# Attention loop without the turned outputs and the output product, in a vision transformer block on one core

## The reference, cut to what matters

```python
h = rows
q, k, v = split(layernorm_rows(h) @ [Wq Wk Wv].T)          # 16 heads of 16
q, k = layernorm16(q) * gq + bq, layernorm16(k) * gk + bk
att = softmax(where(causal, q @ k.T, -1e30)) @ v
h1 = h + att @ Wo.T + bo                                    # what the kernel adds
z = layernorm(h1) * gamma + beta
pre = z @ [abel_w, gate_w] + bias                           # 256 + 8 columns
top2 = the two best of 8 experts, softmax of their logits
moe = sum over top2 of weight * (gelu(z @ ew1[e] + eb1[e]) @ ew2[e] + eb2[e])
moe = moe @ expm(gens[0]) @ expm(gens[1]) @ expm(gens[2])   # gens: 3 of 256 x 256
out = residual + gelu(pre) and moe mixed by a sigmoid gate
```

## Time and profile before

| | us |
|---|---|
| median of 3 runs | 359.7 (358.9 to 361.76) |
| the profiled execution | 359.24 |
| its span | 356.7 |
| busy PE | 320.9 (90% of the span) |
| busy DVE | 219.9 (62%) |
| busy ACT | 184.6 (52%) |
| busy POOL | 140.8 (39%) |

### The profile page before, as it was taken

How to read it: one execution, slowest core, us unless ns; L and a number is a source line. 1 busy time by engine, 2 the same in 40 slices (tenths; PEclk the granted TensorE clock), 3 DMA queues, 4 the chain that set the end, 5 groups by cost and what they waited for, 6 DMA issues and landing times.

```text
span 356.7 us, 6514 instructions
## 1 busy us (share of the span) xinstructions
PE 320.9 (90%) x1954; PEld 272.7 (76%) x1954; DVE 219.9 (62%) x590; ACT 184.6 (52%) x432; POOL 140.8 (39%) x147
## 2 busy tenths in 40 slices
PE   5999999729999999987989599999999999998794
PEld 4987556528888888875778498899988999986673
DVE  0275467997789999987888478776322212113674
ACT  0212455846688989855423785243434556550451
POOL 2001815041445665373004248757752644522000
PEclk9999999955799999999999999999999999999999
DMA  8571411123111110009622366535442567641443
GB/s 253 195 275 55 187 56 56 55 91 131 48 47 48 47 46 17 2 1 408 237 90 80 95 210 178 174 108 169 131 157 75 180 193 194 200 137 59 144 145 103
DMA packets 21120, 45.29 MB, mean 127 GB/s; under 512 B 2086, under 2 KB 14436, under 8 KB 20836
## 3 DMA queue, kind: packets, MB, share of 16 engines
q1 hardware_dynamic: 17444, 36.79, 31.3%
q0 software_dynamic: 2496, 6.82, 6.2%
q10 hardware_dynamic: 1152, 1.32, 1.2%
HBM read 37.71 MB, written 7.22 MB: 126 GB/s over the span
## 4 chain that ended last, share of the span: by engine, by line
PE 71%; issue 7%; DMA 6%; DVE 5%; SPq 3%; ACT 3%; POOL 3%; DVEq 0%; POOLq 0%; ACTq 0%
PE banks L1573 11%; PE banks L1582 10%; PE banks L1515 9%; PE banks L1289 7%; PE banks L1430 6%; PE banks L1406 5%; SPq L372 3%; PE banks L1334 3%; PE banks L1448 3%; PE banks L1379 3%; PE banks L1393 3%; DMA qk_sb<-y_rows 3%; PE banks L1486 2%; DMA qn_sb<-z_rows,gidx_sb 2%; PE banks L1417 2%
## 5 line engine op out<-in xcount | busy, mean ns | idle before, releaser
L1573 PE MATMUL banks<-qn_sb,w_sb 128*128 128x128 f32 x416 | 51.1, 276 | 1.2 <-ACT qn_sb L671 1.0
L1573 PEld LDWEIGHTS banks<-qn_sb,w_sb 128*128 128x128 f32 x416 | 48.6, 192 | 2.1 <-ACT qn_sb L671 1.2
L1582 PE MATMUL banks<-w_sb,sq_sb 128*128 x208 | 49.0, 379 | 0.0
L671 ACT ACTIVATE qn_sb<-banks,col_sb 128x128 f32<-128x128 f32 x52 | 21.0, 454 | 43.9 <-PE banks L1560 39.8
L1204 DVE TENSOR_TENSOR pT_sb<-banks,p_sb 128x256 f32<-128x256 f32 x26 | 11.0, 424 | 52.0 <-PE banks L1582 45.9
L484 POOL DMA_INDIRECT y_rows<-pT_sb,sidx_sb x26 | 25.7, 990 | 43.4 <-DVE pT_sb L1204 42.5
L1582 PEld LDWEIGHTS banks<-w_sb,sq_sb 128*128 128x128 f32 x208 | 38.1, 190 | 4.4
L682 ACT ACTIVATE sq_sb<-banks,col_sb 128x128 f32<-128x128 f32 x104 | 32.3, 364 | 16.4 <-PE banks L1573 13.7
L478 POOL DMA_INDIRECT qn_sb<-z_rows,gidx_sb x26 | 27.9, 1073 | 20.5 <-PE banks L1560 11.5
L572 ACT ACTIVATE kc_sb<-banks,col_sb 32x152 f32<-32x152 f32 x66 | 31.0, 470 | 1.1
L1289 PE MATMUL banks<-patch_sb,wtok_sb 128*128 128x252 f32 (+1 forms) x120 | 26.1, 380 | 4.3 <-DMA wtok_sb<-in_w_tok 4.3
(11 more groups left out here) (234 smaller groups left out, 635.2 us busy)
## 6 DMA issues: line engine op xcount, KB each, us to landing
w_sb<-in_w SPq DMA_DIRECT2D x26, 512.0 KB
...
```

Source lines behind the costliest of these rows:

```text
L1573: last = nc.tensor.matmul(bank[2 + 2 * s + c // 2][:, (c % 2) * 128:(c % 2 + 1) * 128], w1_sb[:, w0:w0 + 128], xsT_sb[:, (2 * s + k) * 128 ...
L1582: last = nc.tensor.matmul(bank[6 + s][:, 0:D], hidT_sb[:, s * HID + k * 128:s * HID + (k + 1) * 128], w2_sb[:, ds(e * 4 * D + k * D, D)], ...
```

## The change

- **The loop** no longer turns attention outputs and makes no output product, up to step 8. GpSimd writes each tile's attention output into `h1_sb`, where it stays; `turn_att`, `keep_attT`, `output` and `finish` of tiles 0 to 2 stand in steps 9 and 10, and those of the other eight behind the loop, between the normalised rows and `pre` of the first tiles. Two buffers hold turned outputs, by turns. `output` of a tile waits for the sum of the tile before it, as it did.
- **Keys.** The six blocks of the turned keys (3 images by 2 halves of a head pair) are copied whole, 304 elements each, three on ScalarE and three on VectorE; VectorE's first one goes ahead of ScalarE's last (`k2_kept`). Both halves of the scores now wait for all copies. `turn_k` stands behind `turn_probs`.
- **Order.** VectorE begins a step with `shift`; ScalarE takes an exponential ahead of `keep_pT` and copies keys last.
- **Constants.** The reduction over partitions becomes a product: VectorE puts the partitions' maxima on a diagonal (`most_sb`), TensorE multiplies it by ones, VectorE takes the largest. The three column sums come after tiles 6, 7 and 8. The second half of `newton` moves into step 1, `size_generators` to the end of step 0.
- **More TensorE work.** `busy` makes products of 512 columns whose result nobody reads: one ahead of the first scores, three behind `turn_q(2)`.
- **Behind the loop** the powers' groups are cut at 5 and 9 tiles (before 7 and 10), and all of them, and all `norm_z`, come behind the last step.

Shared names and tiles:

```diff
+most_sb = pT_sb[:, 128:256]
...
+q_kept, ka_kept, kv_kept, k2_kept, v_spread = sem("q_kept"), sem("ka_kept"), sem("kv_kept"), sem("k2_kept"), sem("v_spread")
...
...
+def attT(t):
+    return attT_sb[:, 0:2 * T] if t % 2 == 0 else att_sb[:, 128:128 + 2 * T]
+def k_part(s, i, a):
+    r = slice(32 * i, 32 * i + 32)
+    dst = kc_sb[r, s * CH:(s + 1) * CH].rearrange("p (n a m) -> p n a m", a=2, m=SEQ)[:, :, a, :]
+    return banks[1][r, :].rearrange("p (n m) -> p n m", m=128)[:, :, SEQ * i:SEQ * (i + 1)], dst, r
...
-CUT = (7, 10)
+CUT = (5, 9)
```

GpSimd:

```diff
     def gather_images(t):
-        att, tmp = att_sb[0:T, t % 2 * D:(t % 2 + 1) * D], tmp_sb[0:T, t % 2 * IPT * D:(t % 2 + 1) * IPT * D]
+        att, tmp = h1_sb[0:T, t * D:(t + 1) * D], tmp_sb[0:T, t % 2 * IPT * D:(t % 2 + 1) * IPT * D]
...
         pool.wait_ge(sel_set, t + 1)
-        if t >= 2:
-            pool.wait_ge(att_turned, t - 1)
...
     spread(0)
-    pool.wait_ge(n_part, 1)
-    pool.partition_all_reduce(nrm_sb[:, 7:8], nrm_sb[:, 6:7], 128, bass.bass_isa.ReduceOp.max).then_inc(n_max, 1)
...
     for t in range(NT):
-        if t == NT - 1:
-            powers(1, 0, CUT[0])
...
     gather_images(NT - 1)
+    powers(1, 0, CUT[0])
```

ScalarE:

```diff
-    def keep_k(t, s, a):
+    def keep_k_part(s, i, a):
+        src, dst, c = k_part(s, i, a)
+        return nc.scalar.activation(dst, src, ACT.Identity, scale=col_sb[c, C_GK + a:C_GK + a + 1],
+                                    bias=col_sb[c, C_BK + a:C_BK + a + 1])
+    def keep_k(t, s):
         act.wait_ge(k_turned, t + 1)
-        for i in range(IPT):
-            r, c = slice(32 * i, 32 * i + 32), slice(SEQ * i, SEQ * (i + 1))
-            kc = kc_sb[r, s * CH:s * CH + CH // 2].rearrange("p (n a m) -> p n a m", a=2, m=SEQ)
-            last = nc.scalar.activation(kc[:, :, a, :], bank[2][r, :].rearrange("p (n m) -> p n m", m=128)[:, :, c], ACT.Identity,
-                                        scale=col_sb[r, C_GK + a:C_GK + a + 1], bias=col_sb[r, C_BK + a:C_BK + a + 1])
-        if a == 1:
-            last.then_inc(ka_kept, 1)
+        keep_k_part(s, 0, 0)
+        keep_k_part(s, 0, 1)
+        act.wait_ge(k2_kept, t + 1)
+        keep_k_part(s, 2, 0).then_inc(ka_kept, 1)
...
     def keep_attT(t):
         act.wait_ge(att_turned, t + 1)
-        if behind(t, 1):
-            act.wait_ge(wo_made, t)
-        nc.scalar.activation(attT_sb[:, :], bank[2][:, 0:2 * T], ACT.Copy).then_inc(attT_kept, 1)
+        if t >= 2:
+            act.wait_ge(wo_made, t - 1)
+        nc.scalar.activation(attT(t), bank[2][:, 0:2 * T], ACT.Copy).then_inc(attT_kept, 1)
...
     def attn_step(t, s):
...
             keep_q(t + 2, s)
-            keep_k(t + 2, s, 0)
-        keep_pT(t)
-        if ahead(t, 2):
-            keep_k(t + 2, s, 1)
...
             exp_half(t + 1, 1 - s, 0)
+        keep_pT(t)
+        if ahead(t, 1):
             exp_half(t + 1, 1 - s, 1)
-        if behind(t, 1):
-            keep_attT(t - 1)
+        if ahead(t, 2):
+            keep_k(t + 2, s)
+        if isinstance(t, int) and t == NT - 2:
+            for u in range(3):
+                keep_attT(u)
...
         if t == 9:
-            keep_k(0, 0, 0)
-    keep_k(0, 0, 1)
+            keep_k(0, 0)
...
     exp_half(0, 0, 1)
-    keep_k(1, 1, 0)
-    keep_k(1, 1, 1)
+    keep_k(1, 1)
...
+    for u in range(3, 8):
+        keep_attT(u)
     for t in range(NT):
-        if t == 4:
-            keep_attT(NT - 1)
         keep_zT(t, t % 2)
+        if t < 3:
+            keep_attT(8 + t)
```

VectorE:

```diff
         if n == G - 1:
-            nc.vector.tensor_reduce(nrm_sb[:, 6:7], nrm_sb[:, 0:6], AX.X, ALU.max).then_inc(n_part, 1)
+            link(nc.vector.tensor_reduce(nrm_sb[:, 6:7], nrm_sb[:, 0:6], AX.X, ALU.max))
+            nc.vector.tensor_scalar(most_sb, con_sb[:, K_ID:K_ID + 128], nrm_sb[:, 6:7], None, ALU.mult).then_inc(n_part, 1)
...
+    def keep_k_part(s, i, a):
+        src, dst, c = k_part(s, i, a)
+        return nc.vector.tensor_scalar(dst, src, col_sb[c, C_GK + a:C_GK + a + 1], col_sb[c, C_BK + a:C_BK + a + 1],
+                                       ALU.mult, ALU.add)
     def keep_k(t, s):
...
             dve.wait_ge(scored, 2 * t - 2)
-        for i in range(IPT):
-            r, c = slice(32 * i, 32 * i + 32), slice(SEQ * i, SEQ * (i + 1))
-            kc = kc_sb[r, s * CH + CH // 2:(s + 1) * CH].rearrange("p (n a m) -> p n a m", a=2, m=SEQ)
-            for a in range(2):
-                last = nc.vector.tensor_scalar(kc[:, :, a, :], bank[3][r, :].rearrange("p (n m) -> p n m", m=128)[:, :, c],
-                                               col_sb[r, C_GK + a:C_GK + a + 1], col_sb[r, C_BK + a:C_BK + a + 1], ALU.mult, ALU.add)
-        last.then_inc(kv_kept, 1)
+        keep_k_part(s, 2, 1).then_inc(k2_kept, 1)
+        keep_k_part(s, 1, 0)
+        keep_k_part(s, 1, 1).then_inc(kv_kept, 1)
...
             norm_k(t - 6, t - 6)
+            column_sums(t - 6)
         elif t == 8:
-            column_sums(0)
+            column_sums(2)
...
     variance(1)
-    column_sums(1)
-    column_sums(2)
...
     def attn_step(t, s):
+        if ahead(t, 1):
+            shift(t + 1, 1 - s)
+        if isinstance(t, int) and t == 1:
+            newton(1, 1)
+        if ahead(t, 3):
+            norm_k(t + 3, 1 - s)
...
             keep_k(t + 2, s)
-        if ahead(t, 1):
-            shift(t + 1, 1 - s)
-        if behind(t, 2):
-            finish(t - 2)
-        if ahead(t, 3):
-            norm_k(t + 3, 1 - s)
         if isinstance(t, int) and t == NT - 1:
-            norm_z(0)
-            norm_z(1)
+            finish(2)
         select(t, s)
-        if isinstance(t, int) and t == 8:
-            aggregate(mv2_sb, 0, CUT[0], NT, h1_stats)
-            variances(0, CUT[0])
+        if isinstance(t, int) and t == NT - 2:
+            finish(0)
+            finish(1)
+        if isinstance(t, int) and t == 0:
+            size_generators()
...
     def size_generators():
-        dve.wait_ge(n_max, 1)
...
+    dve.wait_ge(n_max, 1)
+    link(nc.vector.tensor_reduce(nrm_sb[:, 7:8], bank[7][:, 256:384], AX.X, ALU.max))
...
     newton(1, 0)
-    newton(1, 1)
-    size_generators()
...
-    for t in range(2, 5):
-        norm_z(t)
-    finish(NT - 2)
+    finish(3)
+    finish(4)
+    aggregate(mv2_sb, 0, CUT[0], NT, h1_stats)
+    variances(0, CUT[0])
+    finish(5)
+    finish(6)
+    norm_z(0)
+    finish(7)
+    norm_z(1)
+    finish(8)
...
     variances(*CUT)
+    norm_z(2)
     keep_pre(0)
-    norm_z(5)
+    finish(9)
+    norm_z(3)
     keep_pre(1)
-    norm_z(6)
-    finish(NT - 1)
+    finish(10)
...
     variances(CUT[1], NT)
-    for t in range(2, NT):
+    norm_z(4)
+    keep_pre(2)
+    norm_z(5)
+    for t in range(3, NT):
         keep_pre(t)
-        if t + 5 < NT:
-            norm_z(t + 5)
-        top(t - 2)
+        if t + 3 < NT:
+            norm_z(t + 3)
+        top(t - 3)
+    top(NT - 3)
```

TensorE:

```diff
             pe.wait_ge(kv_kept, t)
-        if behind(t, 4):
-            pe.wait_ge(attT_kept, t - 3)
-        if behind(t, 5):
-            pe.wait_ge(h1_added_c1, t - 3)
...
     def scores(t, s):
         pe.wait_ge(q_kept, t + 1)
+        pe.wait_ge(ka_kept, t + 1)
+        pe.wait_ge(kv_kept, t + 1)
         for hf in range(2):
-            pe.wait_ge(ka_kept if hf == 0 else kv_kept, t + 1)
...
-    def turn_att(t, s, more=True):
+    def turn_att(t):
         pe.wait_ge(att_set, t + 1)
-        if more:
-            pe.wait_ge(ka_kept, t + 4)
-        turn_two(bank[2], att_sb[0:T, s * D:(s + 1) * D]).then_inc(att_turned, 1)
-    def output(t, more=True):
+        if t == 0:
+            pe.wait_ge(ka_kept, NT)
+            pe.wait_ge(kv_kept, NT)
+        else:
+            pe.wait_ge(attT_kept, t)
+        turn_two(bank[2], h1_sb[0:T, t * D:(t + 1) * D]).then_inc(att_turned, 1)
+    def output(t):
         pe.wait_ge(attT_kept, t + 1)
-        if more:
-            pe.wait_ge(kv_kept, t + 5)
-        if behind(t, 1):
-            pe.wait_ge(h1_added_c1, t + 1)
+        pe.wait_ge(h1_added_c1, t + 1)
         for k in range(2):
-            last = nc.tensor.matmul(bank[3][0:T, 0:D], attT_sb[:, k * T:(k + 1) * T], wo_sb[:, k * D:(k + 1) * D],
+            last = nc.tensor.matmul(bank[3][0:T, 0:D], attT(t)[:, k * T:(k + 1) * T], wo_sb[:, k * D:(k + 1) * D],
...
         last.then_inc(wo_made, 1)
+    def busy(n):
+        for k in range(n):
+            nc.tensor.matmul(bank[6][:, :], ident, con_sb[:, K_ID:K_ID + 512], start=True, stop=True)
...
     def attn_step(t, s):
...
             turn_q(t + 2, s)
-            turn_k(t + 2, s)
+            if isinstance(t, int) and t == 0:
+                busy(3)
...
         turn_probs(t, s)
-        if behind(t, 2):
-            output(t - 2, ahead(t, 2))
+        if ahead(t, 2):
+            turn_k(t + 2, s)
+        if isinstance(t, int) and t == NT - 2:
+            turn_att(0)
+        if isinstance(t, int) and t == NT - 1:
+            turn_att(3)
+            output(2)
         values(t, s)
```

(25 more changed lines are left out.)

## The result

The changed kernel takes 371.5 us (median of 4 runs, 370.1 to 373.1) where the kernel before takes 360.7 beside it (4 runs, 358.9 to 364.2): ratio 1.029 [1.019, 1.038], slower; that it is slower by 2% or more is not certain. Every ratio compares only the fast executions of both kernels (those at most 1.5% above a kernel's fastest), while a median is that of all its executions. The profiled execution took 373.07 with a span of 371.2.

The account below looks back on a forecast made before the run. VectorE was taken to set the loop's 7.41 us period. A gain of 16.9 by the last values product less 15.1 behind the loop left 1.8: 359.24 - 1.8 = 357.4, given as 357.5 us, range 352 to 366.

Parts of the forecast that it names:

- Head: Everything up to the first values product: it ends at 79.5 instead of 89.5, gain 10.0.
- costs 0.9: Head: without `busy` the scores would wait until 73.8 for the key copies, so the products cost 0.9.
- Step 1: `values(1)` ends at 87.1 instead of 98.0; gain so far 10.9.
- Step 2: `newton` 1.8, `norm(4)` from 87.2 for 1.5, `values(2)` ends at 94.7 instead of 105.4; gain so far 10.7.
- Steps 3 to 8: Loop steps of 6.0 instead of 7.41: six times 1.4 is 8.5, gain so far 19.1.
- VectorE then needs 5.7: Steps 3 to 8: VectorE's work per step without `finish` (0.91), key copies 1.6 instead of 2.38.
- The loop of 6.0: Steps 3 to 8: cycle through two engines: `turn_q` 0.8, `keep_q` 2.2, turned probabilities 0.6, `turn_k` 0.8, values 1.6.
- Rival C: Wide key copies cost as much as two narrow ones: VectorE's step 6.5, +3.6, 361; chance 0.10.
- Steps 9 and 10: Three outputs stand in them: 11.9 instead of 9.7; gain so far 16.9, last values product at 142.7.
- Behind the loop: Last values product to `rank`, with eight outputs: 36.3 instead of 21.2, 15.1 given back, gain left 1.8.
- bank 3 is single: Behind the loop: each output tile is a hand-off, output 1.06, sum 0.42, semaphore 0.15: 1.65 per tile.
- Rival B: The clock falls behind the loop (+10.5 less 2, 366) or in pauses of steps 1 and 2 (+5, 363); chance 0.20.

Follow-up runs that it names:

- head_two: Kernel before plus the new constants and `busy` products only, scale ahead of first `shift`, second half of `newton` ending step 0: 352.8 us, 0.990.
- head_again: `head_two` unchanged, measured once more against the kernel before, in five rounds: 354.1 us, 0.971.
- head_bare: `head_two` without its four `busy` products of 512 columns: 358.9 us, 0.989 to the kernel before.
- norm_fill: Changed kernel with `norm_k` ahead of `shift` from step 2 on and ten more unread products in TensorE's pauses: 361.5 us, 1.012 to the kernel before.
- loop_out: Changed kernel with `norm_k` first and outputs back in the loop, in banks 1 and 0: 358.6 us, 0.995 to the kernel before.
- tail_order: `norm_fill` with the first five tiles' `norm_z` one place earlier on VectorE, six of seven filling products behind the loop left out: 357.3 us, 0.993.

## Why the prediction was wrong

The change was forecast at 357.5 us and took 371.5. `rank` came 14.9 us later than forecast: 5.1 up to values(2), 7.0 in steps 3 to 8, nothing in steps 9 and 10, 2.8 behind the loop. The step that failed is VectorE's sum for the loop: it charged `norm_k` what it had taken beside an idle GpSimd. The second is that the clock was taken as 1.00 throughout.

- **Head: right** to 0.8 us, and it is real: 8.5 of gain carried to `rank` by `head_two`. But "costs 0.9" for `busy` was wrong in sign: in the kernel with the head alone the products save 4.8 us (`head_again` against `head_bare`). The sum took a clock of 1.00 for granted, and these products are what kept it there; so the head came out right in part by luck.
- **Step 1: right** to 1.0.
- **Step 2: failed.** `newton` took 1.6 as charged (1.8). `norm(4)` started at 87.55, not 87.2, and took 2.27, not 1.5, since `norm_k` started 0.05 before it. The pause of 1.95 so made brought the clock down: 0.50 until 98. VectorE, then GpSimd:

```profile
87.50 0.96 DVE L284 TENSOR_TENSOR kn_sb<-qk_sb,wtok_sb 114x768 f32<-114x768 f32 x1
```

```profile
87.55 2.27 POOL L284 TENSOR_TENSOR qn_sb<-qk_sb,wtok_sb 114x768 f32<-114x768 f32 x1 [3.58 <-DVE wtok_sb L875]
```

- **Steps 3 to 8: the step that failed most.** "VectorE then needs 5.7" took `norm_k` at the 0.85 that it had where GpSimd stood idle. Moved beside GpSimd's work, it takes up to 2.19. The prediction had such a cost in its own rows: it names 3.9 for `newton` beside GpSimd, and charges 0.65 instead of 0.33 for a `norm_z` beside it. The loop of 6.0 was there: the first `turn_q` at full clock, 99.83, is followed by the next at 105.83. Then the keys were late by 0.53 and 1.10, and the clock fell again: 7.2 on average. With `norm_k` first and the long pauses filled it is 6.4: from start to start `turn_k` took 0.93 and values 1.77, where I took 0.8 and 1.6. Three wide copies took 1.72, not 1.6; Rival C (6.5) didn't decide.
- **Steps 9 and 10: right** (12.0, forecast 11.9).
- **Behind the loop: near in size, in part by luck.** With the clock up it takes 35.1, 1.2 less than the forecast of 36.3; the fall of the clock adds 4.0 (39.1). The reason given first, "bank 3 is single", is not what makes the rounds; the order on VectorE, which the same paragraph follows, is.
- **The last sum.** 359.24 - 1.8 is 357.4, and with the 0.5 that the prediction adds for the median it should have given 357.9, not 357.5. The 0.4 changes nothing here.
- **Rival B** had the mechanism and a chance of 0.20, as a thing of the tail (366) or of the early steps (363). Both happened, and it added to the turns: removed alone each is worth 4.6 to 4.7 at `rank`, removed together 10.8. The Trainium skill, "TensorE: Matmul & The Clock Gate", section on psum-queue depth-cycling, has small gaps between groups of products that cycle through PSUM banks set the clock swinging. The clock did fall in the tail (0.50 from 164 to 170), but the gaps there were waits for normalised rows from VectorE, and a second bank changed only 0.5; so the tail neither confirms that rule nor speaks against it. The row of 196 to 204, taken as evidence against it, gives a mean over 8 us and not how long one pause was.

What is left of the 14.9 without the two is 4.1: 2.6 up to values(2), 2.5 in steps 3 to 8 and 0.2 in steps 9 and 10, less the 1.2 of the tail. The time, 361.5, would have been within the range of 352 to 366. And it would not have been a gain: `norm_fill` against `head_two` is the change without its head, and without the two costs. It gains 3.1 by the last values product (148.0, 151.1) and pays 13.9 behind it (35.1, 21.2). In the loop an output costs about 1.0 of a step (7.4 in `loop_out`, 6.4 in `norm_fill`); behind it each is a stage in a chain of hand-offs. The better order of `tail_order` takes away more than half of the loss, but not all of it: 29.6 behind the loop, and `rank` at 176.8, against 183.1 in `norm_fill` and 172.3 in `head_two`. The fastest version found is the head alone, `head_two`: 0.990 and 0.971 in two comparisons. With the outputs behind the loop, the best was 0.993 (`tail_order`). A pause of 1.8 us remains in step 2 of `head_two`; a version without it wasn't made.
